# VectorE's statistics behind the low parts of G, GpSimd's bias ahead of the coefficients: a graph layer on one core

## The reference

```
h   = relu(layernorm(x))
rel = sum_e (h_i W1 + e_ij W1' + b1) * (h_j W2 + e_ij W2' + b2)     # masked where adj == 0
A   = softmax_j(rel)
out = x + relu((A h) gcn_w + gcn_b) Wo + bo
```

## Time and profile before

| | us |
|---|---|
| median of 3 runs (lowest, highest) | 393.53 (391.83, 394.35) |
| the profiled execution, its own time | 394.0 |
| its span, first to last instruction | 392.2 |
| TensorE busy | 363.7 (93%) |
| VectorE busy | 290.5 (74%) |
| ScalarE busy | 272.0 (69%) |
| GpSimd busy | 178.9 (46%) |

### The profile page before, as it was taken

How to read it: one execution, slowest core, us unless ns; L and a number is a source line. 1 busy time by engine, 2 the same in 40 slices (tenths; PEclk the granted TensorE clock), 3 DMA queues, 4 the chain that set the end, 5 groups by cost and what they waited for, 6 DMA issues and landing times.

```text
span 392.2 us, 9499 instructions
## 1 busy us (share of the span) xinstructions
PE 363.7 (93%) x3134; PEld 223.1 (57%) x3134; DVE 290.5 (74%) x669; ACT 272.0 (69%) x578; POOL 178.9 (46%) x349
## 2 busy tenths in 40 slices
PE   3988755999999999999999999999999999889986
PEld 3754432656556565656564756565565656465654
DVE  0747885677777878978878777777778879676574
ACT  3236739788786868686969697786868686853733
POOL 2004537818283746556473818182737465540000
PEclk9778989899999999999999999999999999989999
DMA  7971050339393746546363737393837453324033
GB/s 249 282 218 69 14 152 0 82 80 242 83 242 80 214 107 184 138 144 166 122 163 118 177 105 209 80 241 80 241 80 212 109 148 92 108 54 137 27 97 146
DMA packets 82215, 53.87 MB, mean 137 GB/s; under 512 B 45666, under 2 KB 82148, under 8 KB 82196
## 3 DMA queue, kind: packets, MB, share of 16 engines
q1 hardware_dynamic: 81488, 52.64, 49.4%
q10 hardware_dynamic: 644, 0.79, 0.6%
q0 software_dynamic: 64, 0.20, 0.2%
HBM read 17.44 MB, written 12.58 MB: 77 GB/s over the span
## 4 chain that ended last, share of the span: by engine, by line
PE 44%; DVE 19%; ACT 16%; issue 13%; DVEq 2%; DMA 2%; ACTq 2%; POOL 1%; POOLq 0%
PE bank L988 11%; PE bank L989 10%; PE bank L990 10%; ACT h_parts L435 5%; DVE stats L603 5%; ACT bank L576 4%; ACT h_tok L435 3%; PE bank L1228 3%; PE bank L1223 3%; DVE masks L879 2%; DVE g_parts L752 2%; PE bank L1038 2%; DMA x_all<-in_L_gnn_W_b_dram 2%; ACT hg_hi L475 2%; DVE bank L889 2%
## 5 line engine op out<-in xcount | busy, mean ns | idle before, releaser
L390 POOL TENSOR_TENSOR h_parts<-h_tok,h_parts 128x1536 f16<-128x1536 f32 x14 | 43.4, 3101 | 106.0 <-ACT h_parts L435 106.0
L988 PE MATMUL bank<-gw_hi,hT 128*128 128x385 f16 (+2 forms) x204 | 65.8, 327 | 8.1 <-DVE g_parts L752 4.0
L989 PE MATMUL bank<-gw_lo,hT 128*128 128x385 f16 (+2 forms) x204 | 65.3, 325 | 0.0
L990 PE MATMUL bank<-gw_hi,hT 128*128 128x385 f16 (+2 forms) x204 | 65.2, 324 | 0.0
L988 PE MATMUL bank<-wo_hi,z_hi 128*128 128x384 f16 x180 | 58.7, 326 | 0.0
L989 PE MATMUL bank<-wo_lo,z_hi 128*128 128x384 f16 x180 | 58.7, 326 | 0.0
L990 PE MATMUL bank<-wo_hi,z_lo 128*128 128x384 f16 x180 | 58.7, 326 | 0.0
L988 PE MATMUL bank<-hT,m_hi 128*128 128x512 f16 x144 | 55.2, 383 | 1.9 <-DVE hg_lo L674 1.9
L858 DVE TENSOR_TENSOR z_lo<-bank,z_hi 128x512 f16<-128x512 f32 x48 | 33.2, 692 | 31.0 <-ACT bank L470 31.0
L399 POOL TENSOR_TENSOR x_all<-x_all,bo_all 128x1536 f32 (+1 forms) x16 | 55.1, 3445 | 0.1
L989 PE MATMUL bank<-hT,m_hi 128*128 128x512 f16 x144 | 55.1, 383 | 0.0
(11 more groups left out here) (145 smaller groups left out, 727.3 us busy)
## 6 DMA issues: line engine op xcount, KB each, us to landing
x_all<-in_x_dram SPq DMA_DIRECT2D x16, 768.0 KB, 6.2
out_dram<-x_all SPq DMA_DIRECT2D x15, 768.0 KB, 4.0
hg_parts<-hg_lo SPq DMA_DIRECT2D x32, 192.0 KB, 3.3
hg_parts<-hg_hi SPq DMA_DIRECT2D x32, 192.0 KB, 3.4
out_dram<-x_all SPq DMA_DIRECT2D x4, 192.0 KB, 1.9
x_all<-in_L_gnn_W_w_dram SPq DMA_DIRECT2D x1, 576.0 KB, 5.2
x_all<-in_L_gnn_W_w_dram ACTq DMA_DIRECT2D x1, 576.0 KB, 5.7
gcn_raw<-in_L_gnn_gcn_w_dram SPq DMA_DIRECT2D x1, 576.0 KB, 10.5
```

Of the source, the lines that this page charges most:

```text
L390: nc.gpsimd.tensor_tensor(h_parts[:, :, 1, :], h_tok[:, :, :], h_parts[:, :, 0, :], ALU.subtract).then_inc(h_split, 1)
L988: nc.tensor.matmul(dst, lh, rh, start=(c == 0), stop=False)
L989: nc.tensor.matmul(dst, lh, rl, start=False, stop=False)
L990: last = nc.tensor.matmul(dst, ll, rh, start=False, stop=(c == DC - 1))
```

## The change

VectorE's `statistics(s + 2)` moves from the head of a step to behind the three low parts of G. On GpSimd, in every step but 0, the output bias of step s moves ahead of the coefficients of step s+2, so that it stands directly behind `token_low(s + 1)`. Step 0 keeps its order. No instruction is added or removed, and no wait is changed.

```diff
@@ gpsimd
             def iteration(s, prev=True, nxt=True, nxt2=True):
                 if prev and nxt:
                     token_low(s + 1)
-                if nxt2:
+                if not prev:
                     main_coefficients(s + 2)
                 pool.wait_ge(h_ready, 2 * KT * (s + 1))
                 nc.gpsimd.tensor_tensor(x_all[:, s, :, :], x_all[:, s, :, :],
                                         bo_all[:, :, :].broadcast_to([P, KT, D]),
                                         ALU.add).then_inc(x_biased, 1)
+                if prev and nxt2:
+                    main_coefficients(s + 2)
@@ vector
             def iteration(s, prev2=True, nxt2=True):
-                if nxt2:
-                    statistics(s + 2)
                 g_low_part(s, 0)
                 if prev2:
                     attention_high(s)
                 g_low_part(s, 1)
                 g_low_part(s, 2)
+                if nxt2:
+                    statistics(s + 2)
                 if not prev2:
                     attention_high(s, prev2)
                     dve.wait_ge(wo_high, 1)
```

## The result

The change makes the kernel slower: 422.17 us (median of 6 runs, 420.81 to 422.92) against 393.39 (391.83 to 394.35), ratio 1.0766, interval [1.0722, 1.0809]. 416 was forecast, with 409 to 427 as the range. The profiled execution took 421.96 us with a span of 420.0, 27.8 more than the 392.2 of before.

The account below looks back on a forecast made before the run. TensorE, busy 93% of the span, was taken as the bound, losing 0.28 us a step to VectorE's late L752. Forecast: 394.0 + 22.6 (longer steps) + 0.9 - 1.6 (clock falls) = 415.9, so 416 us, range 409 to 427.

Parts of the forecast that it names:

- The copies behind the bias: VectorE's copies L853, steps 2 to 13: one waits 1.02 us for token_low, the other 3.35 for the bias, as in step 14.
- Rival 1: Loop copies slip through before or ahead of the bias; only the 3.4 us gain is left, 390.6 us; 4%.
- The second ring: Loop cycle through copies, statistics, GpSimd's 20 coefficient steps and normalisation: 22.75 us, the longer one, so it sets the step.
- The first ring: Loop cycle through TensorE: aggregation, tile 3 of H, normalisation, next token_low; 21.95 us, forecast not to set the step.
- rival 3: Loop steps: the coefficients don't bind, so a step takes 21.95 us, 405.4 us in all; 8%.
- The clock: TensorE's granted clock: a fall to 0.50 in step 2 (+0.9 us), none in steady steps, step 14's fall lost (-1.6).
- Rival 2: TensorE's clock falls in all loop steps, 426.6 us, or every second one, 421.6 (420 without step 14's); 33%.
- The 0.28 us: TensorE's wait for L752 before hg_tile(0), each loop step: moving the statistics removes it, 3.4 us over 12 steps.

Follow-up runs that it names:

- run 3: The change, with the two copies reading the transposed attention from its PSUM bank instead of its SBUF copy: 386.05 us, ratio 0.9844.
- run 4: The change, with GpSimd's bias made four instructions of 128 x 384 in place of one: 388.24 us, ratio 0.9898.
- run 2: The kernel before, with only GpSimd's bias moved and the statistics left at the head of VectorE's step: 410.31 us, ratio 1.0437.
- run 8: The change, with 16 dependent GpSimd coefficient steps in place of 20 (one refinement of the root left out): 409.61 us, ratio 1.0404.
- run 7: The change, with ten matmuls of 384 columns put into TensorE's wait for the copies, their result overwritten: 418.69 us, ratio 1.0655.
- run 6: The kernel before, with the bias moved right behind token_low, statistics left at the head, copies reading PSUM: 386.56 us, ratio 0.984.
- run 5: The kernel before, with only the two copies reading PSUM in place of SBUF: 388.55 us, ratio 0.989.
- run 1: The kernel before, with only VectorE's statistics moved and GpSimd's bias left behind the coefficients: 394.09 us, ratio 1.0051.

## Why the prediction came out right

**The copies behind the bias.** Right, and the largest part. One row of step 14 in the old trace gave the size (3.35 us), and runs 3 and 4 show the cause: other data to read from, or a shorter neighbour, and the stall is gone or shrinks to the neighbour's length. Rival 1 has nothing left: in every loop step one copy stands until the bias ends, the second one in eight steps and the first one in the four that follow a fall. The prediction left open whether GpSimd could be the one to wait. It can: in step 1 of the kernel before, VectorE's L667 starts at 71.21 and a coefficient instruction of GpSimd that starts behind it takes 1.31 us in place of 0.20, until L667 is over. In both cases the one that started later waited.

```profile
71.21 1.42 DVE L667 SCALAR_TENSOR_TENSOR wo_lo<-x_all,scale,wo_hi 128x1152 f16<-128x1152 f32 x1 [0.67 <-ACT wo_hi L555]
```
```profile
71.38 1.31 POOL L330 TENSOR_TENSOR root_sq<-root 128x4 f32<-128x4 f32 x1
```

In the loop GpSimd's long instruction had started first each time. The Trainium skill explains run 3 (VectorE: DVE Perf Modes, Why PSUM operands drop a tier): the two-port mode needs both SBUF read ports, so an instruction with a PSUM operand can't use it. The trace agrees as far as it shows: 283 ns from PSUM against 222 from SBUF, and no wait. That it is this port which run 3 frees is the page's word; the runs show only that the place read from decides.

**The second ring.** Right, and 0.20 us too short. (Its terms as written, 7.8 + 1.93 + 0.15 + 6.33 + 6.52, add up to 22.73, not 22.75.) By step 3's rows: 118.22 - 110.43 = 7.79 (forecast 7.8); statistics and hand-over 2.01 (2.08); coefficients 120.23 to 126.65, 6.42 (6.33, two of them take 0.25 us in place of 0.20 beside the masks); until ScalarE starts 0.22 (nothing); until `token_low` 6.51 (6.52). The mis-sized term is the hand-over from GpSimd to ScalarE, 0.22 us that the working left out. Over 12 steps: 25.0 in place of 22.6. Runs 2 and 8 show the ring by taking it away.

**The first ring.** 21.95 was too short by 0.43 (run 2), because the working kept two things of step 14. One is the place of the copies: a TensorE that arrives later puts both behind the start of the bias, 0.26 us. The other is the hand-over from the copies to the aggregation, 0.06 us in the written-out step 14 and 0.23 or 0.24 in every loop step; why the loop's is longer stays open. This ring did not bind in the steady step, but it is what rival 3 was priced by: 405 stood there, and run 2, which makes that case, gives 410.

**The clock.** This is the term that failed in its place, and the largest miss. The prediction put a fall at step 2 (+0.9) and none in the steady steps. Step 2 had none after 2.1 us idle, and steps 4, 6, 10 and 12 had one after 2.2, for 4.3 us with their aftermath (run 7 takes 4.4 away). The nearest row, 1.89 us without a fall, was no bound for steps that repeat the gap 12 times, and the 0.20 us that the second ring lacked went into the gap as well: 2.2 us where 2.0 stood. Step 14, with the 2.03 that was forecast, had no fall. Rival 2 was right in part: four of twelve, not all. That step 14 would lose its fall came out: -1.7, forecast -1.6.

**The 0.28 us.** They are gone, as forecast, but the reason given was only half of it. The prediction blamed the statistics at the head of the step. Run 6 leaves them there and the wait is gone; run 5 leaves the bias beside the masks and it stays. The statistics were late because the masks had stood still for 1.4 us before them. Moving either is enough: the statistics in run 1, the bias in run 6.

In sum: 22.6 + 0.9 - 1.6 were forecast; measured were 25.0 + 4.3 - 1.7 and 0.2 in the opening steps. The execution that came to 421.96 was forecast at 415.9. The range held because it had been drawn wide enough for rival 2, whose 420 to 421.6 (a fall in every second step) lies nearer to the result than the forecast does. That nearness is luck: rival 2 had six falls on steps of 22.75 us, the trace has four on steps of 22.95.

The version that beats both is run 3, 386.05 us: the change's order, with the copies taken from PSUM. Run 6 is level with it, 386.56. In either, TensorE has no wait left in the steady steps of the loop.

## What to carry to other kernels

Before GpSimd work is moved, look which of VectorE's SBUF-to-SBUF copies and `tensor_scalar` instructions will stand beside it: each may wait until the running GpSimd instruction ends, so the price is up to that instruction's length, not the copy's. Not every instruction on SBUF does: the statistics take 0.54 us each beside `token_low` and apart from it. Long GpSimd instructions on the path of such copies are worth splitting, or the copy can read PSUM. And where a loop has one step written out without some of its work, its rows show what a reordered loop will do; after pricing a stall, follow the ring once more round for what becomes late behind it.

## What the runs showed of the hardware

- Nearly the same idle stretch before the aggregation was followed by full clock in steps 2, 3, 8 and 9 (2.13, 2.21, 2.22, 2.21 us) and by half the clock in 4, 6, 10 and 12 (2.22, 2.23, 2.23, 2.22). Stretches of 1.6 to 1.7 us were never followed by a fall (the steps after, and runs 2 and 8), nor were those of 2.10 and 2.11 in step 2 of runs 2 and 8. What decides between the cases of 2.2 us stays open.
- Ten useless matmuls in the wait made the kernel faster, 418.69 against 422.17, by keeping the clock: the 12 steps took 275.29 us against 279.71.
- A small VectorE instruction waits as long as a larger one: 128 x 4 elements stood 3.07 us (run 1), a copy of 64 x 256 stood 3.35. But those over 128 x 1 did not wait: L656 took 0.15 us at 61.47, beside the bias of step 0 (60.20 to 63.64), in the kernel before.
- GpSimd's bias is hardly lengthened by the VectorE instruction that waits for it: 3.41 to 3.47 us in all of these kernels that make it one instruction.
